# Seventeen down products a tile, attention ended by pairs, the last addition on GpSimd, and a new order

## What is computed

```python
x = src                                   # (4, 2048, 256), 64 tiles of 128 rows
xn = layernorm(x)
# s: linear attention and an MLP, both with LayerNorm
Q, K, v = elu(xn @ Wq + bq) + 1, elu(xn @ Wk + bk) + 1, xn @ Wv + bv     # 16 heads of 64
KV = einsum('bshd,bshm->bhdm', K, v)
Z = 1 / (einsum('bshd,bhd->bsh', Q, K.sum(1)) + 1e-6)
o = einsum('bshd,bhdm,bsh->bshm', Q, KV, Z).reshape(b, s, 1024)
x1 = ln(xn + o @ Wo + bo) * g1 + be1
s = ln(x1 + gelu(x1 @ W1 + b1) @ W2 + b2) * g2 + be2
# g: a gated FFN whose inputs and weights are rounded to FP4 in blocks of 16
gate, up = q4(xn) @ q4(w_gate).T, q4(xn) @ q4(w_up).T                    # 704 wide
g = silu(q4(silu(gate) * up) @ q4(w_down).T)
return x + s * g
```

## Time and profile before

| | us |
|---|---|
| median of 3 runs (1749.46 to 1750.88) | 1750.65 |
| the profiled execution | 1750.24 |
| its span, first to last instruction | 1748.4 |
| TensorE busy | 1674.7 (96%) |
| VectorE busy | 1321.7 (76%) |
| ScalarE busy | 968.9 (55%) |
| GpSimd busy | 697.6 (40%) |

### The profile page before, as it was taken

One profiled execution on the slowest core, in us unless ns is written; L12 is line 12 of the kernel. 1 busy time (PEld: TensorE's weight loads), 2 busy tenths in 40 slices (PEclk: granted clock), 3 DMA queues, 4 the chain that ended last, 5 costly groups with the idle time before them and its releaser, 6 DMA issues.

```text
span 1748.4 us, 30645 instructions
## 1 busy us (share of the span) xinstructions
PE 1674.7 (96%) x11203; PEld 1488.6 (85%) x11203; DVE 1321.7 (76%) x2698; ACT 968.9 (55%) x1757; POOL 697.6 (40%) x514
## 2 busy tenths in 40 slices
PE   6989999999899999999999999999999999999997
PEld 5768778888789898988998898988899898989896
DVE  6755755546668787979797887979797887879794
ACT  5555655656446555464646465554646464555643
POOL 3543443434133343434443433434333433344344
PEclk9999999999999999999999999999999999999999
DMA  6412312232400101020110102010100201010100
GB/s 202 145 61 68 120 53 97 80 124 73 139 1 1 49 1 49 1 100 6 45 49 1 49 1 100 1 49 2 49 26 25 91 10 49 1 49 1 49 1 24
DMA packets 65962, 89.33 MB, mean 51 GB/s; under 512 B 4235, under 2 KB 50455, under 8 KB 64790
## 3 DMA queue, kind: packets, MB, share of 16 engines
q1 hardware_dynamic: 65814, 87.38, 14.9%
HBM read 53.29 MB, written 34.08 MB: 50 GB/s over the span
## 4 chain that ended last, share of the span: by engine, by line
PE 61%; DVE 19%; issue 4%; ACT 3%; POOL 1%; DVEq 0%; POOLq 0%; ACTq 0%
PE QH L77 8%; PE QH L79 8%; PE QH L78 8%; PE AC L77 5%; PE AC L78 5%; PE AC L79 5%; PE GU L77 4%; PE GU L79 3%; PE GU L78 3%; DVE rl L1817 2%; DVE hb L1671 2%; DVE QH L1808 2%; DVE hb L1673 2%; ACT rh L1134 2%; PE DN L77 2%
## 5 line engine op out<-in xcount | busy, mean ns | idle before, releaser
L2285 POOL TENSOR_TENSOR hb<-hb,rs_h 128x704 f32<-128x704 f32 x64 | 89.0, 1391 | 327.2 <-DVE rs_h L1680 327.2
L1134 ACT ACTIVATE rh<-QH 128x512 fp32r<-128x512 f32 x256 | 150.5, 596 | 105.1 <-DVE QH L1808 103.5
L1823 DVE TENSOR_TENSOR rl<-QH,rh 128x512 fp32r<-128x512 f32 x128 | 85.2, 675 | 129.7 <-ACT rh L1134 103.0
L77 PE MATMUL GU<-wgh,xqh 128*128 128x352 f32 x448 | 148.4, 331 | 6.5 <-DVE hb L1673 4.9
L2290 POOL TENSOR_TENSOR hb<-hb,sn_h 128x704 f32<-128x704 f32 x64 | 89.1, 1392 | 163.9 <-DVE hb L1685 163.9
L78 PE MATMUL GU<-wgl,xqh 128*128 128x352 f32 x448 | 145.4, 324 | 0.0
L79 PE MATMUL GU<-wgh,xql 128*128 128x352 f32 x448 | 145.2, 324 | 0.0
L77 PE MATMUL AC<-Mh,rh 128*128 128x256 f32 x512 | 145.1, 283 | 0.0
L77 PE MATMUL AC<-w2h,rh 128*128 128x256 f32 x512 | 144.5, 282 | 0.0
L1147 ACT ACTIVATE QH<-QH,cols 128x512 f32<-128x512 f32 x128 | 84.6, 661 | 105.8 <-PE QH L79 104.4
L78 PE MATMUL AC<-w2l,rh 128*128 128x256 f32 x512 | 143.1, 280 | 0.0
(11 more groups left out here) (220 smaller groups left out, 5626.0 us busy)
## 6 DMA issues: line engine op xcount, KB each, us to landing
xa<-in_L_attn_src SPq DMA_DIRECT2D x16, 512.0 KB, 4.0
xt_scratch<-xth SPq DMA_DIRECT2D x32, 256.0 KB, 2.5
xt_scratch<-xtl SPq DMA_DIRECT2D x32, 256.0 KB, 3.0
xb<-in_L_attn_src SPq DMA_DIRECT2D x16, 512.0 KB, 3.9
xnTh<-xt_scratch SPq DMA_DIRECT2D x32, 256.0 KB, 4.6
xnTl<-xt_scratch SPq DMA_DIRECT2D x32, 256.0 KB, 5.7
out<-x SPq DMA_DIRECT2D x16, 512.0 KB, 7.0
m_scratch<-mh SPq DMA_DIRECT2D x16, 256.0 KB, 2.4
```

What stands on the lines that cost most here:

```text
L77: e.matmul(outp, lh, rh, start=start, stop=False, skip_group_check=check)
L1134: e.activation(RH[j % 4][:], src, ACT.Copy).then_inc(S[sem], 1)
L1823: e.tensor_tensor(RL[j % 4][:], QH[:, (j % 2) * 512:(j % 2 + 1) * 512], f(RH[j % 4][:]), ALU.subtract).then_inc(S["gel"], 1)
L2285: e.tensor_tensor(hb, hb, spread(rs_h[i % 2][:], 44), ALU.mult).then_inc(S["hin"], 1)
```

## The change

1. **Down product.** The 704 values are turned in blocks of 128 from the start instead of twice 128, 128, 96. That leaves five full blocks and 64 values. These 64 stand twice in h (GpSimd writes a second copy, already scaled, to columns 704 to 767), and the sixth block of the weight holds the h part of w_down in rows 0 to 63 and its l part in rows 64 to 127. Two products replace three there: 17 a tile. The halves of `turn_h` become blocks (0, 1) and (2, 3, 4, 5), and each half is turned once the whole tile is ready.
2. **Attention by pairs.** `at_step` 6 does j = 6 and 7 for tiles a and b, `at_step` 7 the same for c and d; `ln1_add` of the first pair waits for step 6 alone.
3. **Last addition.** `final_add` moves to GpSimd as a plain addition; g2 and be2 are halved once at the start of the main stage.
4. **Banks.** All gate products use GU.
5. **Order.** The lists of TensorE, ScalarE, VectorE and GpSimd in the main stage are new. SP's is not.

```diff
+H_BLOCKS = ((0, 1), (2, 3, 4, 5))
-GU_ORDER = (((0, 1), "GU"), ((0, 0), "GU"), ((1, 0), "QH"), ...
+GU_ORDER = (((0, 1), "GU"), ((0, 0), "GU"), ((1, 0), "GU"), ...
...
             def weight_turn(n):
-            rows, k0 = 96 if kt % 3 == 2 else 128, (kt // 3) * HALF + (kt % 3) * 128
-            return [rd3[:, t, k0:k0 + rows] for t in range(2)], rows, wdh[0:rows, kt, :], wdl[0:rows, kt, :]
+            return [rd3[:, t, min(kt * 128, 576):min(kt * 128, 576) + 128] for t in range(2)], 128, wdh[:, kt, :], wdl[:, kt, :] if kt < 5 else None
...
             def turn_h(i, hf):
-                w.wait_ge(S["hout"], i + 1)
+                w.wait_ge(S["hout"], 2 * i + 2)
...
-                for k in range(3):
-                    c = hf * HALF + k * 128
-                    last = e.transpose(TT[:, k * 128:(k + 1) * 128], HB[i % 3][:, c:c + 128], ident[:])
+                for n, k in enumerate(H_BLOCKS[hf]):
+                    last = e.transpose(TT[:, n * 128:(n + 1) * 128], HB[i % 3][:, k * 128:(k + 1) * 128], ident[:])
...
             def down(i):
-                if i % 4 == 3 and i + 1 < NT:
+                if i % 4 == DN_TILE + 1 and i + 4 - i % 4 < NT:
                     w.wait_ge(S["zi"], 2 * (i // 4 + 1) + 1)
-                for k in range(6):
-                    rows = 96 if k % 3 == 2 else 128
-                    last = mm3(e, DN[:, 0:D], hqh[0:rows, k, :], hql[0:rows, k, :],
-                               wdh[0:rows, k, :], wdl[0:rows, k, :], k == 0, k == 5)
+                for k in range(5):
+                    mm3(e, DN[:, 0:D], hqh[:, k, :], hql[:, k, :], wdh[:, k, :], wdl[:, k, :], k == 0, False)
+                e.matmul(DN[:, 0:D], hqh[:, 5, :], wdh[:, 5, :], start=False, stop=False)
+                last = e.matmul(DN[:, 0:D], hql[:, 5, :], wdh[:, 5, :], start=False, stop=True)
...
             def at_step(g, j):
-                w.wait_ge(S["zh"], 8 * g + j + 1)
-                w.wait_ge(S["zl"], 8 * g + j + 1)
+                n = j + 1 if j < 6 else 8
+                w.wait_ge(S["zh"], 8 * g + n)
+                w.wait_ge(S["zl"], 8 * g + n)
...
-                acc(j, Mh, Ml).then_inc(S["at"], 1)
+                if j < 6:
+                    last = acc(j, Mh, Ml)
+                else:
+                    tiles = (0, 1) if j == 6 else (2, 3)
+                    acc(6, Mh, Ml, tiles)
+                    last = acc(7, Mh, Ml, tiles)
+                last.then_inc(S["at"], 1)
...
             def ln1_add(g, pr):
-                w.wait_ge(S["at"], 8 * g + 8)
+                w.wait_ge(S["at"], 8 * g + 7 + pr)
...
             def h_out(i):
+                e.tensor_tensor(blocks(HB[i % 3][:, 704:768]), hb[:, 40:44, :], spread(sn_h[i % 2][:, 40:44], 4), ALU.mult).then_inc(S["hout"], 1)
+                w.wait_ge(S["hout"], 2 * i + 1)
                 e.tensor_tensor(hb, hb, spread(sn_h[i % 2][:], 44), ALU.mult).then_inc(S["hout"], 1)
...
-                e.scalar_tensor_tensor(x1[g % 2][:], x1[g % 2][:], 0.5, Xb[g % 2][:], ALU.mult, ALU.add).then_inc(S["fo"], 1)
+            def final_add(g):
+                w.wait_ge(S["us"], g + 1)
+                e.tensor_tensor(x1[g % 2][:], x1[g % 2][:], Xb[g % 2][:], ALU.add).then_inc(S["fo"], 1)
...
             for g in range(1, NG):
-                    gate_up(b + 4, 0)
-                    gate_up(b + 4, 1)
-                    turn_xq(g + 1, 1)
+                    gate_up(b + 4, 0)
+                down(c)
```

More of the change, by code:

```diff
@@ L883, in _ @@
             gate_up(4, 1)
-            turn_h(3, 0)
             q_proj(1, 6)
@@ L935, in _ @@
             for g in range(1, NG):
                 a, b, c, d = 4 * g, 4 * g + 1, 4 * g + 2, 4 * g + 3
+                h_proj(g, 0)
+                h_proj(g, 1)
+                gate_up(d, 1)
+                turn_h(b, 0)
+                f_step(g, 0)
+                h_proj(g, 2)
+                turn_h(b, 1)
+                f_step(g, 1)
+                h_proj(g, 3)
+                f_step(g, 2)
+                h_proj(g, 4)
+                h_proj(g, 5)
+                down(b)
+                h_proj(g, 6)
@@ L1369, in _ @@
             gate_tanh(4, 0)
+            z_sign(1)
+            gate_tanh(5, 0)
+            h_hi(3, 0)
+            g_tanh(2)
+            z_hi(1, 0)
+            z_hi(1, 1)
+            h_abs(4)
+            h_hi(3, 1)
+            z_hi(1, 2)
+            xq_hi(1, 1)
+            gate_tanh(5, 1)
             ln_norm("lnb", 0, 0)
@@ new lines, in _ @@
+                gelu(g, 0)
+                gelu_hi(g, 0)
+                if g + 1 < NG:
+                    x_norm(g + 1, 0)
+                h_hi(b, 0)
+                gelu(g, 1)
+                gelu_hi(g, 1)
+                if g + 1 < NG:
+                    x_norm(g + 1, 1)
+                h_hi(b, 1)
+                gelu(g, 2)
+                gelu_hi(g, 2)
+                h_abs(c)
+                gate_tanh(d, 1)
+                gelu(g, 3)
+                gelu_hi(g, 3)
+                gelu(g, 4)
@@ L2061, in _ @@
             q_elu(1, 1)
+            h_lo(2, 0)
+            h_round(3)
+            q_elu(1, 2)
+            x_max(1, 1)
             h_lo(2, 1)
+            q_elu(1, 3)
+            x_scale(1, 1)
+            xq_lo(1, 0)
             g_mul(1)
@@ L2151, in _ @@
                     q_elu(g + 1, 1)
+                h_lo(c, 0)
+                h_round(d)
+                if g + 1 < NG:
+                    q_elu(g + 1, 2)
+                    x_max(g + 1, 1)
                 h_lo(c, 1)
+                if g + 1 < NG:
+                    q_elu(g + 1, 3)
+                    x_scale(g + 1, 1)
+                    xq_lo(g + 1, 0)
                 g_mul(b)
@@ L2400, in _ @@
             h_in(1)
-            h_out(1)
             maps_done(w)
@@ L2413, in _ @@
             x_in(1, 1)
+            x_out(1, 1)
             ln_rstd("lnb", 0)
-            x_out(1, 1)
+            h_in(4)
             x_plus_bo(1)
-            h_in(4)
+            h_out(4)
             x2_affine(0)
-            h_out(4)
+            final_mul(0)
             h_in(5)
-            final_mul(0)
-            h_out(5)
+            final_add(0)
             ln1_rstd(1, 0)
             ln1_rstd(1, 1)
-            h_in(6)
-            h_in(7)
-            x1_residual(1)
-            h_out(6)
             for g in range(1, NG):
                 a, b, c, d = 4 * g, 4 * g + 1, 4 * g + 2, 4 * g + 3
+                h_out(b)
+                x1_residual(g)
+                h_in(c)
+                h_out(c)
+                h_in(d)
                 if g + 1 < NG:
```

622 lines of the change are left out of this document (258 added, 364 removed), and 1 row of the table SIGNALS.

## The result

The changed kernel takes **1795.9 us** (median of 4 runs, 1792.6 to 1796.9), the kernel before 1750.3 beside it (4 runs): ratio 1.0258, 95% interval 1.024 to 1.0275. It is 45 us slower; I had forecast 28 us faster, 1722, with a range of 1703 to 1744.

What follows compares the result with a forecast made beforehand. Bound by TensorE in the long part and VectorE's queue in the short one; 14 periods x (1.5 + 0.3) = 25.2, first group 2.7, end 0.2: 28.1 us less, giving 1722 us, range 1703 to 1744.

Steps and rivals of the forecast that it cites:

- The order, short part: VectorE's list from denominators' read to gate product's release: 2.0 us less, 0.5 of new waits, so 1.5 us shorter a group.
- Shared port: Rival: a GpSimd operation and a rounding pair hold each other, only x_out before h_round(d), long part; 1739 us, chance 0.05.
- GpSimd late ahead of the rsqrt: Rival: final_add ahead of LN1's rsqrt makes GpSimd's list late, delaying LN1, VectorE and TensorE; up to 1782 us, chance 0.09.
- long part: TensorE gets one gate product, gives one down product; with 0.12 from fewer products, 0.3 us shorter a group, no new stall.
- first group: VectorE's 3.47 us wait for x_plus_bo: about 2.6 stays, 0.9 goes; with the 1.8 a group, 2.7 us gained.
- 17 products: Down product with 17 instead of 18: TensorE's work falls 0.47 us a group, but only 0.12 counts directly.
- Turned halves: Turns and splits of h: six turns stay six, 384 + 384 columns become 256 + 512; no difference.
- Last addition: VectorE loses a 1.22 us operation in the long part, where it idles: nothing; GpSimd pays 2.41, 16 times.
- Queues: Final_add ends about 25.3 us after den_sums' end instead of 34.9; the next Xb load starts earlier and costs nothing.
- Gate product in GU: The gate product now waits for the gate_mul before it: costs nothing if VectorE is on time.
- Pairs: Attention's end: ln1_add may start 1.4 us earlier; no gain of their own, they keep the list's gain from being lost.
- products only: Rival: new waits eat VectorE's 2.0 us, only the saved products count; 1743 us, chance 0.12; sign: over 1.5 us short-part idle.

Runs made afterwards that it cites:

- the last experiment: Changed kernel with h_in waiting for zd and LN1's two rsqrt ahead of final_add, then final_add moved to VectorE behind h_round(b): 1744.5 us, ratio 0.9958.
- with both holds off: Changed kernel, on GpSimd h_in of tile a waits for the four zd operations and final_add stands behind LN1's two rsqrt: 1730.9 us, ratio 0.9894.
- even halves: Changed kernel with h_in waiting for zd, final_add behind the two rsqrt, and h in halves of three and three blocks: 1727.8 us, ratio 0.9867.

## Why the prediction was wrong

**The step that failed** is in "The order, short part": h_scale(a) ahead of z_parts was counted as a move without cost ("following TensorE and VectorE down both lists by these spacings"). I walked two lists with durations from the trace of before, and z_parts's 1.47 us came from a place where GpSimd was idle. That it starts h_in, and that h_in and x_plus_bo then run beside z_parts, I did not ask. It is worth 47 us of stretched instructions and, through the stalls of TensorE, the 7.8 of half clock: in place of 1.5 us less, the short part got 2.2 longer.

**The rival Shared port** had the right mechanism at the wrong place and price: "it could only be x_out (1.07) before h_round(d)", at most 17 us back, which is 1739, at a chance of 0.05. I looked for overlaps in the trace of before, and the change made new ones. The Trainium skill's rule cited there (SBUF — State Buffer, Who interferes with whom) is borne out: zd's instructions, with two tensors in SBUF as inputs, are held to the end of a GpSimd operation that reads SBUF, and in the last experiment a VectorE operation that started first held GpSimd's. The overlap I did name is there too, small: 15 rounding instructions of the changed kernel start 0.3 us before x_out's end and take 0.14 us more than 0.88, 2.1 us in all.

**The rival GpSimd late ahead of the rsqrt** did not come about, though its sign did: the rsqrt starts at 1080.78, 0.10 behind final_add's end. But VectorE was not idle there: its 128x2 operation was held by the same final_add, and putting final_add behind the rsqrt gave 5.5 us in one pair of runs (1751.3 to 1745.8) and 10.7 in another, of two chips (1741.6 to 1730.9). In the periods it is 0.4 and 0.5 us, the size of the hold. The sign could not tell late from held.

**The terms, with both holds off** (1730.9; its profiled span is 19.3 us below that of before, against 28.1 predicted; the parts are those of one group's windows):

| term | predicted | measured |
|---|---|---|
| short part, a group | -1.5 | -1.32 |
| long part, a group | -0.3 | +0.15 |
| 14 periods | -25.2 | -16.3 |
| first group | -2.7 | -4.6 |
| end | -0.2 | +1.8 |
| start | 0 | -0.2 |

- *Short part*: right but for the holds. VectorE's work there fell by 1.71 us (2.0 predicted) and its idle time rose by 0.39 (0.5). ln1_add, predicted 23.4 us behind the end of den_sums, stood at 23.9, and 1.3 us before the end of the last attention product, as named among the signs. The statement that VectorE's queue bounds this part holds: what shortened it shortened the kernel.
- *Long part*: wrong by 0.45 in this group; over the middle groups the mean is +0.06 (47.86 to 47.92), so by 0.36. Start to start, f_step grew from 11.29 to 11.68 us a group and q_proj from 11.35 to 11.57, with no wait for another engine there, and why is open. h_out is not among the causes: its 0.38 was sized well (0.4), and "the turns of h stand well behind it" is right in the new order, where no weight load waits for it. In the old order one turn a group stands right behind it.
- *17 products*: 0.10 to 0.12 saved each time, as priced. Alone in the old order the part costs 7.8 us; in the new order it gives nothing with uneven halves and some 4 us with even ones. The reading that only one product a group counts directly (0.12) missed that the layout has a price.
- *Turned halves*: "no difference" is right in the old order (1758.7 and 1757.4), and 0.37 a group off in the new one, nearly all of it in the short part (30.58 to 30.23).
- *Last addition*: that it costs "nothing" on VectorE in the long part depends on the place: the last run, which puts it elsewhere than before did, lost 13.5, in part through the load of x. On GpSimd its price was the held 0.43, not its own 2.4. The term *Queues* had it right that an earlier final_add costs nothing there; that a later one would cost is what the last run adds.
- *Gate product in GU*: nearly nothing, as said: TensorE's waits for gate_mul with both holds off are 6.7 us over the middle groups against 4.6 before.
- *Pairs*: a gain of 2.6 alone.
- *First group*: the wait for x_plus_bo is 2.4 (2.6 predicted).
- *The signs*: the long part is 47.9 in the changed kernel and with both holds off, so the 48 that I had set as refuting my reading of the order was not passed, though the 0.3 us did not come. With both holds off VectorE's stretch is 30.1 (30 named as right), but its idle time in the short part is 1.63, over the 1.5 named for "products only", while the list's gain did come: that sign was too tight. The periods named as right (77.6 to 78.1) were reached, to 0.03, only with even halves, 78.13.

## What to carry to other kernels

When a step moves, ask what it releases on the other engines and which instructions these will run beside; VectorE instructions with all operands in SBUF deserve that question beside any GpSimd operation, and a duration taken from a place where GpSimd was idle is only a lower bound. A busy engine whose busy time grew while its instruction count fell has stretched instructions: list one line's min, median and max before looking at waits. If such a hold is found, one wait on the side that is early (here GpSimd) is the cheap cure. Ask the same of the DMA queue: an engine's idle time is free only for a step that no load waits for.

## What the runs showed of the hardware

- At z_parts each GpSimd operation held one VectorE instruction to 0.15 us after its own end: 0.34 us became 1.41 and 2.32. No GpSimd operation was held there. The hold also goes the other way: final_add on VectorE (128x1024, two inputs in SBUF), started 0.16 us before GpSimd's 128x64 operation, held it to 0.15 us after its own end, 1.21 us instead of 0.29.
- Not every instruction that overlaps GpSimd is held. In the changed kernel from 560 us on, all that overlap by half their length or more keep their time when one operand is in PSUM (gate_mul 74 times, 0.51; z_mul 60 times, 0.69), and so do two kinds in SBUF alone, the maximum L1673 (30 times, 0.88) and BATCH_NORM_AGGREGATE (30 times, 0.17). The Trainium skill says the same of reductions and of instructions with one SBUF input (SBUF — State Buffer, Who interferes with whom).
- A TENSOR_SCALAR of only two columns, with one SBUF input, is held (0.17 to 0.60). The same section counts tensor_scalar among the operations that can take the shared pair; the trace agrees.
- With a 2.6 us stall of TensorE in each group the granted clock fell to 0.50 in or just behind it in five groups and not in the others, at the same place of the program; it made the 47 us of stretched instructions 7.8 dearer. With stalls of 5.9 to 6.0 us it fell in all 15 groups.
